# Message passing on a graph: the order of the first three tiles, and fourteen scatter groups of three instead of twelve

## The reference

```
h    = max(layernorm(x), 0)                       # per row, eps 1e-5
m    = relu(concat(h[src], h[dst]) @ W.T + b)     # 12500 x 512
out  = x + segment_sum(m, src)                    # 50000 x 512
```

## Time and profile before

| what | us |
| --- | --- |
| median of three runs | 733.67 |
| the profiled execution | 734.02 |
| its span | 732.0 |
| PE busy | 707.6 (97%) |
| DVE busy | 628.2 (86%) |
| POOL busy | 375.0 (51%) |
| ACT busy | 342.4 (47%) |

### The profile page before, as it was taken

One profiled execution on the slowest core, in us unless ns is written; L12 is line 12 of the kernel. 1 busy time (PEld: TensorE's weight loads), 2 busy tenths in 40 slices (PEclk: granted clock), 3 DMA queues, 4 the chain that ended last, 5 costly groups with the idle time before them and its releaser, 6 DMA issues.

```text
span 732.0 us, 12594 instructions
## 1 busy us (share of the span) xinstructions
PE 707.6 (97%) x3466; PEld 586.6 (80%) x3466; DVE 628.2 (86%) x1868; ACT 342.4 (47%) x646; POOL 375.0 (51%) x306
## 2 busy tenths in 40 slices
PE   3999999999999999999999999999999999999995
PEld 2778888888888888888888888888888888888874
DVE  5879999889989989988988998988888888888973
ACT  4444553544445455354445535445444445454441
POOL 6742232323333233232127777777777768877444
PEclk9999999999999999999999999999999999999998
DMA  8999999999999999999977878778787878878665
GB/s 259 383 391 358 391 372 339 374 357 353 391 339 380 343 370 371 341 386 347 349 192 141 140 144 150 152 133 162 137 143 146 137 138 147 159 154 160 86 86 73
DMA packets 36042, 182.46 MB, mean 249 GB/s; under 512 B 7019, under 2 KB 7343, under 8 KB 33049
## 3 DMA queue, kind: packets, MB, share of 16 engines
q0 software_dynamic: 29792, 77.00, 50.0%
q1 hardware_dynamic: 5824, 104.87, 37.9%
q10 hardware_dynamic: 392, 0.20, 0.1%
HBM read 156.44 MB, written 128.09 MB: 389 GB/s over the span
## 4 chain that ended last, share of the span: by engine, by line
PE 94%; DMA 2%; DVE 2%; issue 1%; another core or an unknown queue 0%; POOL 0%; ACT 0%; SPq 0%; DVEq 0%; POOLq 0%
PE z_ps L635 24%; PE z_ps L644 24%; PE z_ps L641 24%; PE ht_ps L618 11%; PE agg_ps L650 5%; PE agg_ps L651 5%; DMA ring<-w_chunks 1%; DMA xg<-x,node_i 1%; DVE ht_lo L313 1%; DVE m_lo L385 0%; DMA node_i<-node_cols 0%; POOL out L236 0%; DVE zb L334 0%; POOL xg L213 0%
## 5 line engine op out<-in xcount | busy, mean ns | idle before, releaser
L213 POOL DMA_INDIRECT xg<-x,node_i x196 | 211.3, 1078 | 245.8 <-PE ht_ps L618 201.2
L635 PE MATMUL z_ps<-w_hi,ht_hi 128*128 128x512 f32 x784 | 315.9, 403 | 1.7 <-DVE zb L323 1.5
L644 PE MATMUL z_ps<-w_hi,ht_lo 128*128 128x512 f32 x784 | 308.9, 394 | 0.0
L641 PE MATMUL z_ps<-w_lo,ht_hi 128*128 128x512 f32 x784 | 307.1, 392 | 0.0
L498 ACT CAST ht_hi<-ht_ps 128x512 fp32r<-128x512 f32 x194 | 104.7, 590 | 299.3 <-PE ht_ps L618 290.9
L236 POOL DMA_INDIRECT out<-ring,add_i x98 | 158.1, 1613 | 104.6 <-DMA out<-ring,add_i 53.3
L644 PEld LDWEIGHTS z_ps<-w_hi,ht_lo 128*128 128x128 f32 x784 | 147.8, 189 | 32.8 <-DVE ht_lo L451 0.2
L635 PEld LDWEIGHTS z_ps<-w_hi,ht_hi 128*128 128x128 f32 x784 | 148.1, 189 | 31.7 <-issue 2.8
L641 PEld LDWEIGHTS z_ps<-w_lo,ht_hi 128*128 128x128 f32 x784 | 148.1, 189 | 30.0
L313 DVE TENSOR_TENSOR ht_lo<-ht_ps,ht_hi 128x512 fp32r<-128x512 f32 x194 | 124.6, 684 | 8.1 <-ACT ht_hi L498 5.6
L505 ACT ACTIVATE xg<-xg,neg_mean 128x512 f32<-128x512 f32 x194 | 129.2, 720 | 2.0 <-DVE neg_mean L287 2.0
(11 more groups left out here) (56 smaller groups left out, 285.8 us busy)
## 6 DMA issues: line engine op xcount, KB each, us to landing
out<-x SPq DMA_DIRECT2D x125, 800.0 KB
xg<-x,node_i POOLq DMA_INDIRECT x196
ring<-w_chunks SPq DMA_DIRECT2D x4, 512.0 KB
out<-ring,add_i POOLq DMA_INDIRECT x98
row_lanes<-src_rows ACTq DMA_DIRECT2D x49, 4.0 KB
bias_bc<-bias SPq DMA_DIRECT2D x1, 256.0 KB, 9.9
node_i<-node_cols SPq DMA_DIRECT2D x1, 98.0 KB, 2.0
```

What stands on the lines that cost most here:

```text
L213: nc.gpsimd.indirect_dma_start(out=xg[:, b, s, :], out_offset=None, in_=x, in_offset=bass.IndirectOffsetOnAxis(ap=node_i[:, column:column ...
L635: nc.tensor.matmul(z_ps[s][:, :], hi, w_hi[:, c, :], start=(k == 0), stop=False)
L641: nc.tensor.matmul(z_ps[s][:, :], hi, w_lo[:, c, :], start=False, stop=False)
L644: last = nc.tensor.matmul(z_ps[s][:, :], lo, w_hi[:, c, :], start=False, stop=(k == KD - 1))
```

## The change

It has two parts. In the written out start:

- Loads 2 and 3 of the weights wait for side 0 of tile 0 only.
- On DVE the statistics of tile 1 follow the first `w_lo` chunk, and its means the first low part; those of tile 2 and 3 come earlier too. Both halves of tile 0 are scaled before the statistics of tile 3. `same_source(0)` and `lanes(0)` move behind `first_half(1)`. DVE now makes six `w_lo` chunks and POOL two.
- On ACT tile 1 is centred before the casts of weight chunks 4 to 7, and `message_high(0)` stands before `high_parts(2)`.
- The half sums of tile 1 go to `agg_ps` instead of `z_ps` (`half_sum`). So the products of tile 1 wait for no half sum, those of tile 2 wait for those of tile 0, and the sums of the first pair wait for `biased` 2.

And 14 groups of three stand in the place of 12: groups of two end at tile 53 (27 of them).

```diff
-    TRIPLES = 12
+    TRIPLES = 14
-    W_POOL = 5
+    W_POOL = 6
+        def half_sum(t, s):
+            return agg_ps[s] if isinstance(t, int) and t == 1 else z_ps[s]
 # sync, ahead of weight load 2
-                    for side in range(SIDES):
-                        sp.wait_ge(first_arrived[side], 16)
+                    sp.wait_ge(first_arrived[0], 16)
 # vector
             first_moments(0, first_mean)
             first_moments(1, mean_ready)
-            w_low_parts(0, 2)
+            w_low_parts(0, 1)
+            statistics(1, 1)
             first_low_part(0)
-            w_low_parts(2, 3)
+            aggregate(1, 1)
+            w_low_parts(1, KD)
             first_low_part(1)
-            w_low_parts(3, KD)
-            statistics(1, 1)
-            aggregate(1, 1)
             w_low_parts(KD, W_POOL)
+            statistics(2, 2)
+            low_parts(1, 1)
             scales(1, 0)
+            aggregate(2, 0)
             dve.wait_ge(bias_loaded, 16)
+            first_half(0, 0)
+            second_half(0, 0)
+            statistics(3, 3)
+            aggregate(3, 1)
+            low_parts(2, 0)
+            message_low(0, 0)
+            first_half(1, 1)
             dve.wait_ge(consts, 4)
             dve.wait_ge(src_cast, 8)
-            for s in range(0, 3):
-                step(s, s)
+            same_source(0, 0)
+            lanes(0, 0)
+            scales(3, 1)
+            step(2, 2)
 # scalar
-            w_high_parts(KD, K)
             deviations(1)
             centre(1, 1)
-            for s in range(0, 3):
-                step(s, s)
+            w_high_parts(KD, K)
+            high_parts(1, 1)
+            centre(2, 2)
+            message_high(0, 0)
+            high_parts(2, 0)
+            deviations(3)
+            centre(3, 3)
+            step(2, 2)
 # tensor, products (its matmuls write half_sum(t, s))
-                    if not (isinstance(t, int) and t == 0):
-                        pe.wait_ge(half_scaled if s == 0 else biased, t)
+                    if not (isinstance(t, int) and t < 2):
+                        pe.wait_ge(half_scaled if s == 0 else biased, 1 if isinstance(t, int) and t == 2 else t)
 # tensor, sums_of_pair
                 if not isinstance(t, int) or t >= 2:
                     pe.wait_ge(ring_filled, t)
+                else:
+                    pe.wait_ge(biased, 2)
```

More of the change, by code:

```diff
@@ L48, in gnn_message_passing_kernel @@
     assert N % COPY_ROWS == 0 and COPIES % COPY_SLOTS == 0 and TILES % 8 == 2 and RING % 8 == 4 and OUT == D and D == 512
-    assert FIRST_ADD <= RING + 4 <= TILES - 12 and FIRST3 >= RING + 4 and FIRST3 % 2 == 0 and TRIPLES % 2 == 0
+    assert FIRST_ADD <= RING + 4 <= TILES - 12 and FIRST3 >= RING + 2 and FIRST3 % 2 == 0 and TRIPLES % 2 == 0
     ctx = ExitStack()
@@ L322, in first_half @@
                 dve.wait_ge(half_done, t + 1)
-                nc.vector.scalar_tensor_tensor(out=zb[:, :], in0=z_ps[0][:, :], scalar=rstd[:, q, b, 0:1],
+                nc.vector.scalar_tensor_tensor(out=zb[:, :], in0=half_sum(t, 0)[:, :], scalar=rstd[:, q, b, 0:1],
                                                in1=bias_bc[:, :], op0=ALU.mult, op1=ALU.add).then_inc(half_scaled, 1)
@@ L333, in second_half @@
                     dve.wait_ge(stats_done, SIDES * (t + 4))
-                nc.vector.scalar_tensor_tensor(out=zb[:, :], in0=z_ps[1][:, :], scalar=rstd[:, q, b, 1:2],
+                nc.vector.scalar_tensor_tensor(out=zb[:, :], in0=half_sum(t, 1)[:, :], scalar=rstd[:, q, b, 1:2],
                                                in1=zb[:, :], op0=ALU.mult, op1=ALU.add).then_inc(biased, 1)
@@ L634, in products @@
                             pe.wait_ge(w_hi_ready, c + 1)
-                        nc.tensor.matmul(z_ps[s][:, :], hi, w_hi[:, c, :], start=(k == 0), stop=False)
+                        nc.tensor.matmul(half_sum(t, s)[:, :], hi, w_hi[:, c, :], start=(k == 0), stop=False)
                         if early:
@@ L640, in products @@
                                 pe.wait_ge(w_rest_ready, c - W_POOL + 1)
-                        nc.tensor.matmul(z_ps[s][:, :], hi, w_lo[:, c, :], start=False, stop=False)
+                        nc.tensor.matmul(half_sum(t, s)[:, :], hi, w_lo[:, c, :], start=False, stop=False)
                         if early and k == 0:
                             pe.wait_ge(lo_ready, s + 1)
-                        last = nc.tensor.matmul(z_ps[s][:, :], lo, w_hi[:, c, :], start=False, stop=(k == KD - 1))
+                        last = nc.tensor.matmul(half_sum(t, s)[:, :], lo, w_hi[:, c, :], start=False, stop=(k == KD - 1))
                     last.then_inc(half_done if s == 0 else mm_done, 1)
```

## The result

The changed kernel takes 736.69 us in the median of 18 runs, the kernel before 733.76 us beside it. The ratio is 1.0041, with a 95% interval of 1.0024 to 1.0058: some 3 us slower. Forecast were 732.7 us and a range up to 735.7. On another chip the ratio was 1.0043 [1.0001, 1.0085], and on a third 0.9985 [0.9954, 1.0015]; what differed between the chips is part of what follows.

What follows compares the result with a forecast made beforehand. PE was taken to bound the kernel from tile 3's products on. Groups of three at +1.34 us and those products starting 2.4 us earlier summed to -1.1 us, giving 732.7 us, with a range from 731.0 to 735.7.

Steps and rivals of the forecast that it cites:

- The groups of three: PE's path in the loops: fourteen groups instead of twelve add six matmuls, costing 1.34 us.
- The weight loads: Start, SP's queue: loads 2 and 3 are issued 0.6 us earlier and taken to land 0.6 us earlier.
- between 11 and 13 us: Start: when tile 1 is in memory, by queue bytes; its transposes then start around 17 instead of 18.91.
- DVE's chain: Start, tile 3's statistics to tile 1's `m_lo`: begins at 25.0, takes 11.3 instead of 13.92 us, ends 2.6 us earlier.
- bound for late data: Start: if tile 2 lands as late as before (20.95), DVE's stretch starts at 26.7 and gains 0.9 us.
- The unnamed wait: 2.92 us before DVE's first half of tile 2, no engine named; taken as tied to that place, moving with DVE.
- a fetch: Beside the loop's start: possible instruction fetch with full DMA queues behind the 2.92 us stall; no row shows it.
- the stall goes: Rival, chance 0.2: no stall before tile 2's first half; tile 3's products start at 38.9 to 39.2, time 731.1 us.
- The rival of a start that doesn't pay: Chance 0.25: tile 2's first half released at a fixed time, tile 3's products at 43.0; 735.0 to 736.7 us.
- The forecast fall from 20 to 24 us: PE's old clock fall, mean 0.52 from 20 to 23.5 us, costing 1.7 us; granted clock forecast at 1.00 there.
- The rival of a fall behind the new wait: Chance 0.15: PE's clock falls after new idle times in the start, costing 0.5 to 1.7 us; 733.2 to 734.4.
- The chain of adds: POOL's adds: 1.96 us to spare, 2.4 us shorter with fourteen groups; rival that they bound, chance 0.02, 731.3 us.

Runs made afterwards that it cites:

- e7_copies_late: The changed kernel with SP's copies of x held back until the third tile's low message is made; 1208.6 us at a mean granted clock of 0.56.
- e6: The changed kernel as it is, run again on another chip, against the kernel before; ratio 1.0043 [1.0001, 1.0085].
- e12: The changed kernel as it is, run a third time on a third chip, against the kernel before; ratio 0.9985 [0.9954, 1.0015].
- e5_both_14: The changed kernel, fourteen groups included, but weight loads 2 and 3 wait for both sides of tile 0; ratio 0.9984 [0.9965, 1.0003].
- b1_before_again: The kernel before, unchanged, run once more for its profile; no time given, tile 7 transposed at 61.15 us.
- b2_before_third: The kernel before, unchanged, run a third time on a chip with late copies; no time given, tile 7 transposed at 59.72 us.
- e1: The kernel before with fourteen groups of three instead of twelve, its start untouched; ratio 0.9981 [0.9963, 0.9999].
- e4: The changed kernel with twelve groups, DVE making tile 0's first low part ahead of tile 1's statistics, early loads kept; ratio 1.0008 [0.9976, 1.0039].
- e3: The changed kernel with twelve groups, weight loads 2 and 3 waiting for both sides of tile 0; ratio 1.0000 [0.9966, 1.0033].
- e13: The kernel before with one edit, weight loads 2 and 3 waiting for side 0 of tile 0 alone; ratio 1.0004 [0.9976, 1.0031].
- e9: The changed kernel, fourteen groups, with weight loads 2 and 3 waiting for both sides of tile 0 and tile 1's gather; one time, 736.31 us.
- e2_start_only: The changed kernel with its new start but twelve groups of three as before; ratio 1.0007 [0.9980, 1.0035].

## Why the prediction was wrong, step by step

**The groups of three: right.** From tile 50 to tile 97 PE needs 338.29 to 338.38 us in each profile with twelve groups and 339.67 to 339.70 in each with fourteen, e7_copies_late left out: 1.3 to 1.4 us more; forecast 1.34.

**The weight loads: the step that failed.** The prediction gave them a gain of 0.6 us and saw that they share the queues with tile 1's gather, but priced that only for the weights. It took tile 1 to be in memory "between 11 and 13 us" from the bytes of the earlier trace rows, which are those of the old issue times, and called its place "not what decides". In the new order the runs put tile 1's statistics at 13.8 to 15.5 with the early loads and at 10.7 to 12.4 without. The low parts and weight chunks that tile 0's products need stand behind it on DVE; tile 1 was transposed at 20.28 where the forecast had 17.

**DVE's chain: its length about right, its start mis-sized.** Forecast were a start at 25.0, from tile 2's statistics at 18.5 to 19.3 and 5.7 us of work behind them, and a length of 11.3 us. Measured with the change were tile 2's statistics at 19.96 to 21.78, the chain's start at 26.5 to 27.2, 5.4 to 6.9 us behind them (up to 1.1 us of it waiting for tile 1's high parts), and, without an unnamed wait, lengths of 11.6 (e6) and 12.4 us (e12). So it was the landing of the gathers that the sum had wrong, and not DVE's work. With the loads held back the start was at 25.14 and `m_lo` ended at 36.76, where the prediction had 36.3: the start that was forecast is that of e5_both_14, which the change is not. Its bound for late data, a start at 26.7 and a gain of 0.9 us, was the one that came true, and it stood in no case of the sum.

**The unnamed wait: wrong.** It was tied to an instruction of DVE ahead of the loops. It belongs to no instruction: it was 0.9 to 6 us long, at DVE, ACT and POOL, in six of the sixteen profiles above; b1_before_again and b2_before_third, the same program as the first, are without it. How it falls is striking: all six profiles from the first two sets of runs (the two kernels, and e1 to e4) have it, and none of the eleven from the three chips used later, whatever the kernel. So it goes with the chip or the time rather than with single executions; which, and why, is open. The old trace also has no packet of an instruction queue from 39 to 42.2 us, so that nothing bears out a fetch. Where the wait is 2.9 us or more it costs either start 3 to 4 us (63.50 against 60.4, 65.20 and 64.68 against 61.1, 61.88 against 58.8), not more in the changed one than the spread of these numbers. As rival ("the stall goes") it was a case of the kernel, when it should have been a spread around both.

**The rival of a start that doesn't pay: near in its number, by luck.** Its 735.0 to 736.7 us came from a release of tile 2's first half at a fixed time. No profile of the change has such a wait there; what the profiles show is a chain that starts late with the gathers, and in the first one an unnamed wait at another place.

**The clock.** The forecast fall from 20 to 24 us is gone. The rival of a fall behind the new wait came true in the changed kernel's profile: after 1.99 us of idle PE tile 4's transposes took 1.91 us; in e6_change_again, after 1.54 us, they took 1.04. The half rate up to 20 us, which PE's rows show behind its stop at tile 0, stood in no case.

**The chain of adds: its weight wrong, its shortening not shown.** The prediction found 1.96 us to spare and gave the rival in which the adds end the kernel 0.02. Where the copy ends 4 to 8 us later they do end it (b2, e3 and e13 with twelve groups, e1 and e9 with fourteen). There e1's ratio of 0.9981 [0.9963, 0.9999] says that fourteen groups don't cost what they cost PE; the chains' lengths scatter too much to say how much they give.

The sum by the measured terms: +1.4 us of the groups, +0.7 (means without an unnamed wait, of two profiles each) to +1.7 us (the two first profiles; b2 and e12 have 1.6) of the start, 2.1 to 3.1 us together; timed were 3.0 us [1.8, 4.3]. The start's part rests on few profiles, and no old start was profiled on the chip of e5 and e6. Whether the rest of the timed loss is late signals that weigh more on the changed order isn't shown: that would need many profiles on one chip that has them.

## What to carry to other kernels

A transfer that is issued earlier can take the queues from those in flight: ask of each whose data the next engine in line stands waiting for, and price the change there. When work is moved ahead in an in-order queue, everything behind it inherits its latest input, so look for when that input lands in the new traffic, not in the old. Where two chains end within a fraction of a per cent of each other, look at both on more than one chip before buying time in one with time of the other. The best version of these is the new order with weight loads 2 and 3 waiting for both sides and fourteen groups, at 0.9984 [0.9965, 1.0003] and 0.9980 [0.9947, 1.0013]; it isn't proved faster than the kernel before.

## What the hardware did that I had not expected

ACT, DVE and POOL were released together up to 5 us behind the rows of PE for which they waited, within the first 45 us only, and in two sets of runs out of five; the cause is open. In e7_copies_late the clock stayed between its two levels of 1.2 and 2.4 GHz in the mean, at 0.56, for 1.2 ms with PE busy throughout; one window of it, with the columns of the earlier trace rows:

```profile
60.00:200.00 140.00, 140.00 (x414) 84.11 (x413) 74.97 (x218) 41.79 (x78) 29.11 (x24) 0.56 0.99 350
```

It was one execution, and nothing here shows what set it off. And single gathers in the middle of the kernel landed so late that DVE waited for them: 3 times and 7.1 us in e5_both_14, 11 times and 20.6 us in e2_start_only, never in the two first profiles. PE feels it: from tile 7 to tile 50 it takes 304.54 to 304.56 us in the eight profiles without such waits, and 2 to 16 us more in the other eight (e7_copies_late left out), 4.3 us more in e5_both_14, whose last transposes are therefore later than e6_change_again's (707.38 and 705.12). That may be why single times of one kernel lie 6 us and more apart.
